# Attention's output rows transposed later and into another bank, the maxima sent from ScalarE, and the variance one tap earlier

## The chip, the cores and the metric

The kernel runs on one core of one Trainium2 chip. The metric is the device time of one execution in microseconds (us), the median over runs. TensorE (PE) multiplies, VectorE (DVE), ScalarE (ACT) and GpSimd (POOL) do elementwise work, SyncE (SP) issues transfers. Each engine runs its own instruction list in order and waits on semaphores for the others.

## What is computed

The input is x, four images of 96 channels and 128 x 128 pixels, float32. Two layers follow each other. Cut to what matters:

```python
# layer 0
xn = layernorm over the 96 channels of each pixel
qk, vs = conv1x1(xn, qk_w), conv1x1(xn, vs_w)            # q, k: 48 channels each, vs: 96
local = depthwise 3x3 conv(vs)
v1, v2 = vs[:, :48], vs[:, 48:]
q, k, v1 = rolled by (-4, -4), cut into 8 x 8 windows, 4 heads of 12 channels
y = softmax(q k^T / sqrt(12)) v1                          # 64 x 64 per window and head
y = concat([windows put back and rolled back, v2])
ca = sigmoid(fu2(leaky_relu(fu1(mean over the image of (y + local)))))
z = conv1x1(y * ca + local * (1 - ca), proj_w) + x
# layer 1: depthwise conv with 4 taps, whose weights come from the image mean of z
out = conv of z with w(relu(batchnorm(w1 @ mean(z)))) + bias
```

Both layers need a mean over a whole image (for `ca` and for layer 1's weights) before the first row of that image's output can be finished.

## The kernel before

The 128 rows of an image are cut into 16 strips of 8 rows (`NS`), 64 strips in all. A strip goes through two parts.

*Attention* of strip t: x is loaded, transposed (`x_transposed`, L471, in two halves) and its statistics taken (`statistics` L980, `variance` L986 to L994); `rsqrt` (L758, L762) and `rstd_rows` (L483) give the factors by which `normalise` (L1001) makes `xn`. From `xn` come values (`vs_of` L496, copied out by `vs_out` L780) and keys and queries (`keys_queries` L504, copied out by L767 or L1210 and by L773). `scores` (L521) makes q k^T of half of the windows in `banks_s`; `maxima` (L1009) takes row maxima, a reduction for each of the two banks; `max_transposed` (L535) turns them, `maxima_out` (L806 on ScalarE, L1017 on VectorE in the first 16 strips) negates them into `nmx`, and SyncE's `move_max` (L281) sends them into rows 62 to 65 of `qd`, where they serve as extra rows of the next product. `scores_transposed` (L529) makes k q^T minus the maxima in both banks of `banks_t`, `exps` (L811) exponentiates from there into `pt`, `values` on TensorE (L558) multiplies by `vd` into `ps_o` (first half) or bank 0 of `banks_t` (second half), `divide` (L1024, L1026) normalises into `yq`. `y_transposed` (L541) transposes `yq` into `ps_o`, ScalarE's `y_out` (L799, four copies, and L801) copies it into `ybuf`, SyncE's `store_y` (L296) writes it to DRAM as `y_img`. The values go to DRAM as `v_img` through GpSimd (L434).

*Mixing* of strip u = t - 17 (`LAG`), one image behind: SyncE's `load_strip` loads `vin`, `ycat`, rows of `mixed` and x0, seven transfers; ScalarE's `first` (L837) and six taps on VectorE (`mix`, L1181) make the local convolution, `project` and `project_mixed` (L612, L614, L619) multiply into `banks_g`, `finish` (L1204) adds x0 and writes `zs`, ScalarE's `tap0` (L847) and three taps on VectorE (`l1`, L1192) make layer 1, and `store_out` writes the result.

The order of instructions on each engine is written out by hand: `alone` for the first 16 strips (attention alone), `strip` for the 48 in which both parts overlap and for the 16 of mixing alone that follow (the last of these on VectorE by `last`). `gate` marks the strip after an image's last, in which the sums over the image are taken (`image_sums` on ScalarE, L882 and L883, `local_mean` and `squeeze_in` on VectorE, from L1108), `gated` the strip after it, in which the image's weights are made.

What orders the work around the change, within one overlapped strip:

- TensorE: x transposes first half, transposed scores first half (waits for `mx_moved`), values' projection (waits for `zs_done`), `y_transposed(t - 1)`, transposed scores second half (waits for the first exponentials), x transposes second half, keys and queries, weighted sums first half, `rstd_rows`, scores first half, project first half, scores second half (waits for the first maxima), weighted sums second half, `max_transposed`, project second half, values transposed, `project_mixed`.
- ScalarE: exponentials first half, `vs_out`, `y_out(t - 1)`, exponentials second half, keys, `rsqrt`, queries, `tap0`, sums of x, `maxima_out`, `first`, values.
- VectorE: `finish`, statistics first half, three taps, statistics second half, variance, two taps, divide, normalise, maxima first half, one layer 1 tap, maxima second half, last tap, divide, two layer 1 taps.
- SyncE: store of the output, `store_y(t - 1)`, two loads of x, two stores of values, `load_strip`, `move_max`.

## Time and profile before

| | |
|---|---|
| runs, median | 1499.13 us (1495.72 to 1505.75, 3 runs) |
| the profiled execution's own time | 1503.79 us, its span 1502.2 us |
| mean granted TensorE clock | 0.984 |
| strips of attention alone | the first 16, to about 300 us |
| strips with both parts | 48, to about 1307 us |
| strips of mixing alone | the last 16 |

The profile is one execution. A line of the timeline gives the start and the duration of an instruction or a run of equal ones, the engine, the line of the kernel, and in brackets how long the engine idled before it and which instruction released it. PEld is TensorE's loading of weights, which overlaps its multiplying. The granted clock is a share of 2.4 GHz.

### The profile page before, as it was taken

The page shows a single profiled execution, that of the slowest core. Times are in us where ns is not written, and L with a number is a line of the kernel's source. Part 1 is how long each engine was busy: PE and PEld are TensorE (multiplying, and loading weights), DVE is VectorE, ACT ScalarE, POOL GpSimd, SP SyncE. Part 2 cuts the span into 40 slices and gives each one's busy share as a digit, 9 for nine tenths or more (in the row PEclk, how much of TensorE's full clock was granted, in tenths as well). Part 3 has the DMA queues.
Part 4 walks back from the last instruction along what each step waited for, and adds up shares of the span by engine and source line. Part 5 has one row for each costly group of instructions (what it writes and reads, how often), then busy time and mean ns, then how long its engine had stood idle before and what let it go on. Part 6 is the DMA issues. An engine that isn't in the chain of part 4 may idle for free.

```text
span 1502.2 us, 38208 instructions
## 1 busy us (share of the span) xinstructions
PE 1323.6 (88%) x12403; PEld 782.0 (52%) x12403; DVE 1263.8 (84%) x2222; ACT 875.8 (58%) x2279; POOL 230.8 (15%) x741
## 2 busy tenths in 40 slices
PE   5989898889899999989899999988989998888986
PEld 3666666555555555555555555555555555433332
DVE  3565656479999999999999999999989998999998
ACT  2566666666666666776566666765666666622221
POOL 2111111111122211221111211220112011000000
PEclk9999999999999999999999999999999999999999
DMA  2121212345665566645655566646655664678884
GB/s 62 51 82 55 81 55 81 99 98 148 167 148 144 138 152 165 156 114 154 166 147 139 138 159 156 156 114 159 155 125 141 161 155 112 164 181 195 211 199 126
DMA packets 81357, 203.07 MB, mean 135 GB/s; under 512 B 15248, under 2 KB 19112, under 8 KB 81320
## 3 DMA queue, kind: packets, MB, share of 16 engines
q1 hardware_dynamic: 81320, 202.60, 53.9%
q8 instruction: 20, 0.33, 0.1%
q14 instruction: 17, 0.14, 0.0%
HBM read 136.57 MB, written 64.91 MB: 134 GB/s over the span
## 4 chain that ended last, share of the span: by engine, by line
PE 36%; ACT 20%; DVE 16%; issue 13%; DMA 13%; ACTq 1%; DVEq 0%; SPq 0%; POOL 0%; POOLq 0%
DMA qd<-nmx 12%; PE banks_s L521 9%; ACT pt L811 5%; PE banks_t L529 5%; PE banks_t L483 5%; ACT km L767 4%; DVE mx L1009 4%; ACT ybuf L799 4%; PE banks_g L612 4%; PE banks_g L496 4%; DVE mixed L1181 3%; PE banks_g L614 3%; DVE oo L1192 3%; ACT vw L780 2%; DVE zs L1204 2%
## 5 line engine op out<-in xcount | busy, mean ns | idle before, releaser
L1181 DVE SCALAR_TENSOR_TENSOR mixed<-vin,c_pack,mixed 96x1024 f32<-96x1024 f32 x352 | 450.0, 1278 | 6.6
L1192 DVE SCALAR_TENSOR_TENSOR oo<-zs,l_w,oo 96x1024 f32<-96x1024 f32 x192 | 245.1, 1276 | 8.3 <-ACT oo L847 4.1
L811 ACT ACTIVATE pt<-banks_t 128x512 f32<-128x512 f32 x256 | 138.6, 593 | 129.0 <-PE banks_t L529 127.5
L1009 DVE TENSOR_REDUCE mx<-banks_s 128x8 f32<-128x512 f32 x260 | 167.6, 687 | 48.1 <-PE banks_s L521 47.3
L529 PE MATMUL banks_t<-qd,km 64*128 64x128 f32 x2048 | 152.8, 290 | 30.1 <-DMA qd<-nmx 30.0
L521 PE MATMUL banks_s<-km,qd 64*128 64x128 f32 x2080 | 152.9, 286 | 18.9 <-issue 15.2
L980 DVE BATCH_NORM_STATS2 bn<-banks_a 128x6 f32<-128x96 f32 x528 | 99.0, 249 | 80.5 <-PE banks_a L471 80.1
L521 PEld LDWEIGHTS banks_s<-km,qd 64*128 64x128 f32 x2080 | 129.7, 189 | 70.7 <-DVE mx L1009 40.4
L612 PE MATMUL banks_g<-vin,proj_t 128*96 128x512 f32 (+1 forms) x288 | 150.2, 622 | 11.4 <-DMA ycat<-y_img 5.7
L529 PEld LDWEIGHTS banks_t<-qd,km 64*128 64x128 f32 x2048 | 127.9, 192 | 49.9 <-issue 26.1
L434 POOL COPY vrow<-vw 96x16 f32<-96x16 f32 (+2 forms) x520 | 153.4, 349 | 0.0
L847 ACT ACTIVATE oo<-zs,c_pack,l_w 96x1024 f32<-96x1024 f32 x64 | 79.0, 1235 | 125.7 <-DVE zs L1204 125.7
L429 POOL TENSOR_TENSOR idle<-idle 96x1 f32<-96x1 f32 x65 | 34.2, 527 | 767.2 <-ACT vw L780 767.2
L789 ACT ACTIVATE vd<-banks_a 64x192 f32<-64x192 f32 x260 | 86.8, 334 | 109.9 <-PE banks_a L510 104.8
L496 PE MATMUL banks_g<-xn,c_pack 96*96 96x512 f32 x260 | 136.6, 650 | 5.7 <-DVE zs L1204 4.4
L504 PE MATMUL banks_g<-xn,w_qk 96*32 96x512 f32 x1040 | 126.8, 605 | 0.0
L483 PE MATMUL banks_t<-ident,rstd 128*96 128x128 f32 x528 | 72.2, 281 | 50.0 <-ACT rstd L762 31.7
L614 PE MATMUL banks_g<-ycat,proj_c 128*96 128x512 f32 x224 | 115.3, 596 | 0.0
L619 PE MATMUL banks_g<-mixed,proj_m 128*96 128x512 f32 x224 | 109.2, 610 | 1.6 <-DVE mixed L1181 1.6
L806 ACT ACTIVATE nmx<-banks_s 32x128 f32<-32x128 f32 x48 | 12.8, 266 | 163.4 <-PE banks_s L535 163.4
L780 ACT ACTIVATE vw<-banks_g,vs_bias 96x512 f32<-96x512 f32 x130 | 88.6, 682 | 27.2 <-PE banks_g L496 22.9
L799 ACT ACTIVATE ybuf<-banks_a 48x256 f32<-48x256 f32 x256 | 93.9, 370 | 4.2 <-PE banks_a L541 2.7
(148 smaller groups left out, 1842.5 us busy)
## 6 DMA issues: line engine op xcount, KB each, us to landing
vin<-v_img SPq DMA_DIRECT2D x64, 495.0 KB, 5.9
v_img<-vrow SPq DMA_DIRECT2D x130, 198.0 KB, 2.8
xc<-in_x SPq DMA_DIRECT2D x134, 192.0 KB, 2.6
x<-in_x SPq DMA_DIRECT2D x64, 384.0 KB, 7.2
out<-oo SPq DMA_DIRECT2D x64, 384.0 KB, 3.0
y_img<-ybuf SPq DMA_DIRECT2D x128, 99.0 KB, 2.0
ycat<-v_img SPq DMA_DIRECT2D x64, 198.0 KB, 4.9
ycat<-y_img SPq DMA_DIRECT2D x64, 198.0 KB, 7.0
```

The lines of the kernel that those rows point to most:

```text
L434: nc.gpsimd.tensor_copy(dst.rearrange("c r (p x) -> c p r x", x=min(WS, src.shape[-1])), src).then_inc(vrow_done, 1)
L483: last = nc.tensor.transpose(bc_bank(c)[:C, j * W:(j + 1) * W], rstd[:, at:at + 1].to_broadcast([128, C]), ident[:])
L496: mm(banks_g[:C, w, :], wvs[:], windows(w), start=True, stop=True).then_inc(vs_done, 1)
L521: last = mm(banks_s[:, t, e * 128:(e + 1) * 128], operand(qd, t, k, p), operand(km, t, k, p), start=True, stop=True, tile_position=(64 * t ...
L529: last = mm(banks_t[:, n, e * 128:(e + 1) * 128], operand(km, n, k, p), operand(qd, n, k, p), start=True, stop=True, tile_position=(64 * n ...
L612: mm(z, proj_t[:rows, n, :], vin[:rows, par, at:at + 4, 1 + dw:1 + dw + W], start=n == 0, stop=False)
L614: mm(z, proj_c[:], ycat[:, par, 4 * c:4 * c + 4, 0:W], start=False, stop=False)
L799: fn(dst, src[:, :, wi, :, :], ACT.Copy, accum_out=ystat[0:A, bass.ds(4 * t + 2 * g + wi, 1)]).then_inc(y1_done, 1)
L811: fn(pt[:, 2 * r + n, :], banks_t[:, n, :], ACT.Exp).then_inc(pt_done, 1)
L1009: v.tensor_reduce(mx[:, n, :, 4 * r:4 * r + 4].rearrange("q h e -> q e h"), banks_s[:, n, :].rearrange("q (e h k) -> q e h k", h=2, k=K), ...
L1181: v.scalar_tensor_tensor(out=mb[:C, par, :, 0:W], in0=vin[:C, par, 1 + dh:1 + dh + WS, 1 + dw:1 + dw + W], scalar=depth_w[:, DVE_TAPS[m]:D ...
L1192: v.scalar_tensor_tensor(out=oo[:, par, :, :], in0=zs[:, at:at + WS, 1 + dw:1 + dw + W], scalar=l1_w[:, n:n + 1], in1=oo[:, par, :, :], op ...
```

## The change

It has six parts.

1. `y_transposed(t - 1)` moves on TensorE from behind the values' projection to behind the second half of the weighted sums, ahead of `max_transposed`, and writes bank 1 of `banks_t` in place of `ps_o`. `yq` gets two buffers. The wait on `y1_done` moves from `values` to ahead of the transposed scores' first half. In overlapped strips the second half of the x transposes takes the free place, ahead of the second half of the transposed scores.
2. `y_out` moves on ScalarE to behind the sums of x (in overlapped strips also behind `maxima_out`), ahead of the values.
3. In overlapped strips ScalarE itself issues the transfer of the maxima behind `maxima_out`, and SyncE no longer does. In the first 16 strips SyncE still issues it. `store_y` becomes the last item of SyncE's strip (in a `gate` strip it stands ahead of the load of `y_img`).
4. `maxima` is one reduction over both banks in place of two, and its semaphore counts 2 a strip in place of 4.
5. On VectorE the second half of the statistics and the variance go ahead of the third tap, on ScalarE `rsqrt` ahead of the keys.
6. In a `gate` strip ScalarE's image sums go behind `maxima_out` and `y_out`, and VectorE's `local_mean` and `squeeze_in` behind the last layer 1 tap.

The core of the diff:

```diff
-        yq = sb("yq", [128, 4, 2, 64])
+        yq = sb("yq", [128, 2, 4, 2, 64])
...
                 if gate is not None:
+                    if rows is not None:
+                        store_y(rows, 1 - rows_par)
                     sp.wait_ge(y_stored[1], FREE + 32 * (NS // 2) * (gate + 1))
...
-                if y:
+                if y and not attend:
                     store_y(t - 1, 1 - k)
...
-                if attend:
+                if attend and alone:
                     move_max(t + 1, 1 - k)
+                if y and attend and gate is None:
+                    store_y(t - 1, 1 - k)
...
-            def y_transposed(t):
-                pe.wait_ge(vd_done, 4 * (t + 2))
+            def y_transposed(t, k):
                 pe.wait_ge(yq_done, FREE + 2 * (t + 1))
                 for e in range(4):
-                    last = nc.tensor.transpose(ps_o[:, e * 128:(e + 1) * 128],
-                                               yq[:, e, :, :].rearrange("q g c -> q (g c)"), ident[:])
+                    last = nc.tensor.transpose(banks_t[:, 1, e * 128:(e + 1) * 128],
+                                               yq[:, k, e, :, :].rearrange("q g c -> q (g c)"), ident[:])
...
                 vs_of(t + 1)
-                if y:
-                    y_transposed(t - 1)
                 x_transposed(t + 2, k, h + 1, 0)
                 pe.wait_ge(mx_moved, 16 * (t + 1))
                 pe.wait_ge(yq_done, FREE + 2 * t)
+                if not (isinstance(t, int) and t < 2):
+                    pe.wait_ge(y1_done, YO * (t - 1))
                 scores_transposed(k, 0)
...
-                values(t, k, 1, not y)
+                values(t, k, 1)
+                if y:
+                    y_transposed(t - 1, 1 - k)
                 pe.wait_ge(yq_done, FREE + 2 * t + 1)
                 max_transposed(t + 1)
...
                     pe.wait_ge(yq_done, FREE + 2 * t)
+                    pe.wait_ge(y1_done, YO * (t - 1))
                     scores_transposed(k, 0)
                     if prev:
                         pe.wait_ge(zs_done, u)
                     vs_of(t + 1)
+                    x_transposed(t + 2, k, h + 1, 1)
...
                 if attend:
-                    x_transposed(t + 2, k, h + 1, 1)
                     keys_queries(t + 1)
...
-                    values(t, k, 1, not y)
+                    values(t, k, 1)
+                    y_transposed(t - 1, 1 - k)
...
-            def maxima_out(s):
+            def maxima_out(s, k):
                 act.wait_ge(mt_done, s + 1)
                 act.wait_ge(mx_moved, 16 * s)
                 fn(nmx[:], ps_mx, ACT.Copy, scale=-1.0).then_inc(nmx_done, 1)
+                act.wait_ge(nmx_done, s + 1)
+                act.dma_start(qd[62:66, k, :, :, :].rearrange("j p w q -> j (p w q)"), nmx[:]).then_inc(mx_moved, 16)
...
+                    rsqrt(t + 2)
                     keys(t + 1, 1 - k)
-                    rsqrt(t + 2)
                     queries(t + 1, 1 - k)
...
                     sum_x(t + 2, k, h + 1, 0)
                     sum_x(t + 2, k, h + 1, 1)
+                if attend:
+                    maxima_out(t + 1, 1 - k)
+                    y_out(t - 1, 1 - k, h - 1 + k)
                 if gate is not None:
                     image_sums(gate)
-                if attend:
-                    maxima_out(t + 1)
...
-                for n in range(2):
-                    v.tensor_reduce(mx[:, n, :, 4 * r:4 * r + 4].rearrange("q h e -> q e h"),
-                                    banks_s[:, n, :].rearrange("q (e h k) -> q e h k", h=2, k=K),
-                                    AX.X, ALU.max).then_inc(mx_done, 1)
+                v.tensor_reduce(mx[:, :, :, 4 * r:4 * r + 4].rearrange("q n h e -> q n e h"),
+                                banks_s[:, :, :].rearrange("q n (e h k) -> q n e h k", h=2, k=K),
+                                AX.X, ALU.max).then_inc(mx_done, 1)
...
                     mix(u, par, 0, tail)
                     mix(u, par, 1, tail)
+                if attend:
+                    statistics(t + 2, 1)
+                    variance(t + 2)
                 if gated is not None and attend:
                     leaky(gated)
                 if cur:
                     mix(u, par, 2, tail)
-                if attend:
-                    statistics(t + 2, 1)
-                    variance(t + 2)
```

## Rows read from the trace of the kernel before

**Rows 1.** The page: the chain that ended last, by line.

```profile
DMA qd<-nmx 12%; PE banks_s L521 9%; ACT pt L811 5%; PE banks_t L529 5%; PE banks_t L483 5%; ACT km L767 4%; DVE mx L1009 4%; ACT ybuf L799 4%; PE banks_g L612 4%; PE banks_g L496 4%; DVE mixed L1181 3%; PE banks_g L614 3%; DVE oo L1192 3%; ACT vw L780 2%; DVE zs L1204 2%
```

**Rows 2.** Busy time, 665 to 959 us: us, each engine's busy us (x instructions), clock.

```profile
665.00:959.00 294.00, 267.22 (x2646) 159.66 (x2644) 273.22 (x449) 190.63 (x483) 54.65 (x154) 1.00 0.59 149
```

**Rows 3.** Windows of L1181 alone (six taps to a strip): stretch, us, busy us (x).

```profile
328.00:620.00 292.00, 107.51 (x84) 1.00 0.60 149
665.00:959.00 294.00, 107.20 (x84) 1.00 0.59 149
1004.00:1286.00 282.00, 99.57 (x78) 0.98 0.58 144
```

**Rows 4.** Waits, 665 to 959 us: who for whom; us in total, times, longest.

```profile
PE banks_t L529 <- DMA qd<-nmx: 7.4, 12, 1.2
DVE mx L1009 <- PE banks_s L521: 7.0, 15, 0.5
DVE zs L1204 <- PE banks_g L619: 6.6, 14, 0.6
...
DVE bn L980 <- PE banks_a L471: 2.3, 6, 0.7
```

**Rows 5.** Timeline, one strip's end: start, us, engine, line, operation, [idle before <-releaser].

```profile
742.08 1.29 DVE L1009 TENSOR_REDUCE mx<-banks_s 128x8 f32<-128x512 f32 x2 [0.51 <-PE banks_s L521]
...
743.43 0.28 PE L535 MATMUL banks_s<-ident,mx 128*32 128x128 f32 x1 [0.34 <-DVE mx L1009]
...
744.12 0.67 SPq L281 DMA_DIRECT2D qd<-nmx  x1
...
748.18 1.28 DVE L1204 SCALAR_TENSOR_TENSOR zs<-banks_g,z_bias,x 96x1024 f32<-96x1024 f32 x1 [0.56 <-PE banks_g L619]
...
749.55 1.16 PE L529 MATMUL banks_t<-qd,km 64*128 64x128 f32 x16 [1.25 <-DMA qd<-nmx]
```

**Rows 6.** Timeline, the strip after it, up to the first maxima.

```profile
752.44 0.60 PE L541 MATMUL banks_a<-ident,yq 128*128 128x128 f32 x4
...
753.41 0.36 ACT L799 ACTIVATE ybuf<-banks_a 48x256 f32<-48x256 f32 x1
...
755.19 1.08 ACT L811 ACTIVATE pt<-banks_t 128x512 f32<-128x512 f32 x2
...
759.59 1.16 PE L521 MATMUL banks_s<-km,qd 64*128 64x128 f32 x16 [0.33 <-issue]
...
760.78 1.29 DVE L1009 TENSOR_REDUCE mx<-banks_s 128x8 f32<-128x512 f32 x2 [0.25 <-PE banks_s L521]
```

**Rows 7.** Timeline: the maxima's transfer issued, and the product that waits for it.

```profile
279.18 0.68 SPq L281 DMA_DIRECT2D qd<-nmx  x1
...
281.22 2.08 PE L529 MATMUL banks_t<-qd,km 64*128 64x128 f32 x16 [1.36 <-DMA qd<-nmx]
```

**Rows 8.** A window of low clock: us, then busy us by engine, clock.

```profile
1263.00:1270.00 7.00, 6.77 (x26) 3.89 (x28) 3.73 (x3) 2.64 (x6) 0.05 (x1) 0.51 0.02 6
```

**Rows 9.** Timeline: the second statistics' wait just after that window.

```profile
1271.54 0.76 DVE L980 BATCH_NORM_STATS2 bn<-banks_a 128x6 f32<-128x96 f32 x4 [4.74 <-PE banks_a L471]
```

**Rows 10.** Timeline: maxima in a strip where VectorE, not TensorE, is late.

```profile
654.68 1.28 DVE L1009 TENSOR_REDUCE mx<-banks_s 128x8 f32<-128x512 f32 x2
...
657.24 1.29 DVE L1009 TENSOR_REDUCE mx<-banks_s 128x8 f32<-128x512 f32 x2
```

**Rows 11.** Timeline, one strip of the first 16, attention alone.

```profile
204.04 0.28 PE L535 MATMUL banks_s<-ident,mx 128*32 128x128 f32 x1 [0.34 <-DVE mx L1009]
...
209.55 1.08 ACT L811 ACTIVATE pt<-banks_t 128x512 f32<-128x512 f32 x2
```

**Rows 12.** Timeline: ScalarE's image sums, first and last, and VectorE's use of them.

```profile
632.49 0.22 ACT L882 ACTIVATE spare<-vstat 96x32 f32 x1
...
634.33 0.20 ACT L883 ACTIVATE edge<-ecol 96x4 f32 x1
...
637.48 0.15 DVE L1108 TENSOR_TENSOR edge<-edge 96x9 f32<-96x9 f32 x1
```

More of the change, by code:

```diff
@@ L344, in _, with strip @@
             move_max(0, 0)
-            def strip(h, k, attend=True, y=True, ahead=False, prev=False, older=False, gate=None):
+            def strip(h, k, attend=True, y=True, ahead=False, prev=False, older=False, gate=None, alone=False):
                 t = 2 * h + k
@@ L591, in _ @@
             scores(0, 0)
-            pe.wait_ge(mx_done, 2)
+            pe.wait_ge(mx_done, 1)
             scores(0, 1)
@@ L661, in strip @@
                     vs_of(t + 1)
+                    x_transposed(t + 2, k, h + 1, 1)
                 elif prev:
                     pe.wait_ge(zs_done, u - 1 if tail and gated is None else u)
-                if y:
-                    y_transposed(t - 1)
+                if y and not attend:
+                    pe.wait_ge(y1_done, YO * (t - 1))
+                    y_transposed(t - 1, 1 - k)
                 if gated is not None:
@@ L674, in strip @@
                 if attend:
-                    x_transposed(t + 2, k, h + 1, 1)
                     keys_queries(t + 1)
-                    values(t, k, 0, not y)
+                    values(t, k, 0)
                     rstd_rows(t + 2, 0)
@@ L684, in strip @@
                     pe.wait_ge(mid_act, gated + 1)
+                    if not attend:
+                        pe.wait_ge(y1_done, YO * B * NS)
                 if attend:
@@ L912, in strip @@
                     vs_out(t + 1, 1)
-                if y:
+                if y and not attend:
                     y_out(t - 1, 1 - k, h - 1 + k)
@@ L1292, in strip @@
                     l1(u - 1, k, 3)
+                if gate is not None and attend:
+                    local_mean(gate)
+                    squeeze_in(gate)
                 if gated is not None:
```

47 lines of the change are left out of this document (21 added, 26 removed).

## Prediction

> **What bounds the kernel now.** I read the page first, then busy time by stage, the waits of the middle stage, the timeline of one of its strips, and the timeline of the first 16 strips. The page says that the largest item of the chain is no engine but the transfer `qd<-nmx` (12%) [rows 1]. Averages hide three stages: 16 strips of attention alone, 48 in which attention of one image overlaps the mixing of the image before, and 16 of mixing alone. The change acts on the first two.
>
> In the middle stage, six taps make a strip: 84 taps are 14 strips, so a strip takes 292/14 = 20.9 us, then 294/14 = 21.0, then 282/13 = 21.7 [rows 3]. VectorE is busy for 273.2/14 = 19.5 us of the 21.0 and TensorE for 267.2/14 = 19.1 [rows 2]. So the most that any reordering could take out is about 1.5 us a strip. Of VectorE's idle 1.48 us, the waits explain 1.14: before the maxima 7.0, before `zs` 6.6, before the second statistics 2.3, together 15.9/14 [rows 4]. The other 0.34 are small gaps.
>
> These waits have one source upstream, a loop through all engines: maxima, transposed (L535), negated, sent by `qd<-nmx`, transposed scores (L529), exponentials, values and output rows copied on ScalarE, the second exponentials, keys, `rstd`, scores, maxima. In the strip shown the transfer is issued at 744.12 and the product that needs it starts at 749.55, after 1.25 us of idle TensorE [rows 5]; it waits in 12 of 14 strips [rows 4]. Then the output copies stand on ScalarE between the first and the second exponentials from 753.41 to 755.19, 1.78 us [rows 6]. Scores come at 759.59, VectorE waits 0.25 for them [rows 6].
>
> **The transfer.** SyncE issues it behind seven loads of the next strip. The one issued at 279.18, with nothing large ahead of it, let its product start at 281.22, 2.04 us later [rows 7]; the one at 744.12 took 5.43 [rows 5]. The change issues it from ScalarE in the middle stage (SyncE keeps it in the first). I take 2.0 to 4 us, since it no longer stands in SyncE's order; the bound from above is 5.4. TensorE is free for the product about 0.1 us after `zs` starts (749.55 less 1.25), which is 4.2 us after the issue, so anything under 4.2 is hidden. The issue itself costs ScalarE something that before does not show: SyncE's took 0.67 and 0.68 [rows 5, 7]. I take 0.7. Queued behind it are the output rows, `first` and `vd`, and behind these the next strip's exponentials. From 744.1 + 0.3 the sum is 0.7, 1.78, 1.28 for `first` (1024 columns, as a tap) and at most 1.78 for `vd`'s four copies: 749.9. The exponentials could start at 749.5, when the product is no longer late. They are at most 0.4 late, and TensorE needs the first pair (1.08) only after values' projection and x transposes, at about 752: the issue may cost 1.7 before anything waits.
>
> The Trainium skill speaks against this gain (DMA: Bandwidth & Descriptors, Issuing engines are not separate DMA queues): DMAs from SP and ACT interleave on the same 16 engines, and issuing from several saves only sequencer time. Its section Queues, rings and completion order says that each DMA engine takes turns between rows, packet by packet, which would let a 16 KB transfer past a backlog. The trace has no transfer from ScalarE that could decide; the first reading is rival A.
>
> **Output rows off the loop.** Their transposes (L541, 0.60 us [rows 6]) leave the gap between the value product and the second transposed scores and go behind the weighted sums; the second x transposes take their place, and the copies (1.78 us) move behind the maxima. Second statistics and variance go one tap (107.2/84 = 1.28 us [rows 3]) earlier. The scores were ready 11.4 us after `zs` (759.59 less 748.18); without 1.78 and with the product 1.2 earlier they could be at about 9.7, while VectorE's own work brings it to the first maxima no earlier than about 11.8. VectorE becomes late there, by about 2 us, so the waits before the statistics (2.3/14 = 0.16) and before the first maxima go. The wait before the second maxima shrinks: it was 0.5 because the scores of the first half and the two projections behind them were late. In a strip in which VectorE was the late one, the pair started at 654.68 and 657.24 with no wait noted [rows 10], 2.56 apart, which is the 2.5 of its own work. I keep 0.1.
>
> **What it costs.** The transposes now sit where TensorE idled only 0.34 us, waiting for the maxima (L535) [rows 5]. Of 0.60 us, 0.26 is left over, and every projection up to `zs` comes that much later; the pipelined spacing may be less (bounds 0.1 and 0.6). The wait before `zs` grows from 6.6/14 = 0.47 to 0.7. Two banks of `yq` and bank 1 of `banks_t` add waits on `y1_done` that the copies of the strip before satisfy, over 1 us early.
>
> **Merged maxima.** One reduction over 1024 columns replaces two of 512, twice a strip. A pair takes 1.29 us, and another operation over 1024 columns, `zs`, 1.28 [rows 5]: the saving could be nothing. At most it is a small operation's whole time, 0.15 [rows 12]. I take 0.05, so 0.1 a strip.
>
> **Sum, middle stage.** 19.5 - 0.1 busy, 0.34 small gaps, 0.1 and 0.7 of waits: 20.5 us a strip. Against 20.9, 21.0 and 21.7 that is 0.4 x 14 + 0.5 x 14 + 1.2 x 13 = 28 us. The last term holds a mechanism of its own: after idling for the transfer TensorE ran at half rate (2.08 instead of 1.16 us for the same product [rows 5, 7]); the granted clock from 1263 to 1270 was 0.51, the 1.2 GHz level, after an idle wait for the same transfer [rows 8], and VectorE then stood 4.74 us [rows 9]. I count two such strips in the third stretch, whose clock is 0.98 against 1.00 in the others [rows 3]. With the transfer early, both go.
>
> **Sum, other parts.** First 16 strips: the transposes fill 0.34 us of idle before L535 [rows 11] and leave their old place, and the exponentials at 209.55, which stood behind the output copies, come forward. TensorE's order sets this stage, so I take 0.34 less the unfilled rest, 0.25 (bounds 0.1 and 0.4): 15 x 0.25 = 4 us. The first two overlapped strips both wait for the transfer; the second gets it about 1 us earlier: 2 us. Two strips at an image's end lose: the image sums (632.49 to 634.53, 2 us [rows 12]) now stand behind issue and output copies, VectorE's mean waits for them, and its small steps no longer lie between taps: 0.5 each, -1 us. SyncE there waits for the output rows before it stores them and loads `y`, which is needed 10 us later. The last 16 strips are untouched.
>
> 28 + 4 + 2 - 1 = 33 us off the profiled execution's own 1503.8 gives 1471. The runs' median is 0.3% lower, 1499.1; 33 off that is 1466, but the two half-rate strips (8 us) may belong to the profiled execution alone. I settle at 1469.
>
> **Rivals.** *A, the transfer stays late.* It lands 5.4 us after its issue as now. The product is still about 1.2 us late, but with the copies gone and two us of reserve this reaches VectorE only through the second statistics, which now stand a tap earlier: about 0.3 us over 41 strips, 12 us: 1481. For it: both queues end in the same engines, whose share is 59% [rows 2]. Against: 2.04 us where nothing was ahead. *B, paid back ahead of `zs`.* If the transposes cost their whole 0.60, so that the serial stretch from second maxima to `zs` (6.1 us in rows 5) grows to 6.7, and 0.3 of wait is left before the second maxima, a strip is 20.5 + 0.3 + 0.2 = 21.0. Then -1, 0 and 9 us come from the three stretches and 5 from the other parts, 13 us: 1486, or 1491 if the half-rate strips are the profiled execution's alone; I put 1489. For it: TensorE has 93% of a 20.5 us strip. Against: its idle 0.34 in just that place. *C, slower.* TensorE now runs ahead of VectorE, and its waits could gather in one place ahead of the scores. Half rate followed an idle stretch of 1.36 [rows 7]; one costs about 4.5 us of a strip. It decides from about seven strips more than now (33/4.5); for over 1% slower, eleven: 1515. Against: at 20.5 us all TensorE's idle together is 1.4, in three places of at most 0.7.
>
> **Chances and range.** Forecast 0.66, A 0.12, B 0.16, C 0.06. A 1% difference (15 us) is about what a measurement can tell. Faster by over 1%: forecast, and most of A, 0.78; within 1%: B, 0.16; slower 0.06. The range goes from 1455 (a strip at 20.3, 0.4 gained in the first stage) to 1488, where A and a half of B end; B's rest and C are left out.
>
> **What would show it.** Right: no idle before L529 for the transfer; 20.4 to 20.6 us between `zs`; waits before statistics and first maxima gone, before the second under 0.2, before `zs` 0.6 to 0.8; no clock under 0.9 after 350 us. Wrong: an issue on ScalarE over 1.7 us, exponentials late by it, or waits ahead of `zs` over 1 us.

## The result: slower by 1.1%, and the profile after

| | before | after |
|---|---|---|
| median of 13 runs each | 1500.8 us (1495.72 to 1508.32) | 1518.62 us (1506.93 to 1537.8) |
| ratio | | 1.0112, 95% interval 1.0083 to 1.0140 |
| the profiled execution | 1503.79 us | 1527.75 us |
| its mean granted clock | 0.984 | 0.953 |

The highest run of the kernel after, 1537.8 us, is a slow one and is left out of the ratio. Forecast was 1469 us, in a range from 1455 to 1488. The time is on the other side. The two profiled executions are 24 us apart, the medians 18: the table by stages below shows a larger loss than the usual one.

In the profile after, the chain that ended last gives the transfer less, 8% for 12% [rows 1], and the statistics (L991), which wait for TensorE's transposes, appear in it:

```profile
DVE mixed L1191 12%; DMA qd<-nmx 8%; PE banks_g L500 7%; PE banks_s L525 6%; PE banks_t L559 4%; DVE bn L991 4%; PE banks_g L508 4%; PE banks_t L533 4%; PE banks_g L620 3%; PE banks_g L613 3%; DVE oo L1202 3%; DVE mx L1019 3%; PE banks_g L615 3%; PE banks_t L487 3%; PE banks_t L544 2%
```

The windows of the three overlapped stretches (columns as in [rows 2]) show that they no longer resemble each other. The first keeps full clock; the second and third fall to 0.95 and 0.94, and VectorE's busy time falls from 273.22 [rows 2] to 256.50, since fewer strips fit into the same window:

```profile
328.00:620.00 292.00, 273.48 (x2716) 165.97 (x2720) 275.04 (x436) 198.98 (x500) 63.73 (x157) 1.00 0.61 152
665.00:959.00 294.00, 264.63 (x2493) 158.37 (x2497) 256.50 (x405) 181.17 (x456) 68.76 (x149) 0.95 0.57 140
1004.00:1286.00 282.00, 258.74 (x2436) 155.14 (x2435) 248.48 (x393) 177.09 (x447) 63.27 (x139) 0.94 0.57 140
```

The waits from 665 to 959 us, which answer to [rows 4]. The maxima's wait is gone (7.0 to 1.4), `zs` waits about as before (7.7 for 6.6), but TensorE waits 20.1 us for the transfer instead of 7.4, in 11 strips and for up to 2.7, and the second statistics 23.3 instead of 2.3:

```profile
DVE bn L991 <- PE banks_a L475: 23.3, 8, 3.9
...
PE banks_t L533 <- DMA qd<-nmx: 20.1, 11, 2.7
...
DVE zs L1214 <- PE banks_g L620: 7.7, 13, 0.7
...
DVE mx L1019 <- PE banks_s L525: 1.4, 3, 0.6
```

A strip in which all goes well, in the timeline. The transfer is issued at 748.78 and its product starts 4.12 us later without a wait. `zs` follows again after 20.13 us:

```profile
748.78 0.64 ACTq L816 DMA_DIRECT2D qd<-nmx  x1
...
752.85 1.28 DVE L1214 SCALAR_TENSOR_TENSOR zs<-banks_g,z_bias,x 96x1024 f32<-96x1024 f32 x1 [0.70 <-PE banks_g L620]
752.90 1.16 PE L533 MATMUL banks_t<-qd,km 64*128 64x128 f32 x16
...
757.41 3.02 POOL L438 COPY vrow<-vw 96x256 f32<-96x256 f32 x8
...
758.75 2.79 DVE L1191 SCALAR_TENSOR_TENSOR mixed<-vin,c_pack,mixed 96x1024 f32<-96x1024 f32 x2
```

A strip that takes 23.55 us, and what it hands to the next. Here x0's load is issued 0.11 us ahead of the maxima. The product waits 2.66 us, then runs in 2.00 instead of 1.16 (the granted clock from 707 to 711 us is 0.57), the values' projection in 2.73 instead of 1.93, VectorE stands 3.37 before its second statistics, and GpSimd's eight copies take 5.07 instead of 3.02. SyncE's loads of the next strip stand behind the store of these copies, so that the next x0 load again comes only 0.73 us ahead of the next maxima:

```profile
700.12 0.32 SPq L322 DMA_DIRECT2D x<-in_x  x1
700.23 0.64 ACTq L816 DMA_DIRECT2D qd<-nmx  x1
...
704.27 1.28 DVE L1214 SCALAR_TENSOR_TENSOR zs<-banks_g,z_bias,x 96x1024 f32<-96x1024 f32 x1 [0.67 <-PE banks_g L620]
...
707.05 2.00 PE L533 MATMUL banks_t<-qd,km 64*128 64x128 f32 x16 [2.66 <-DMA qd<-nmx]
708.99 2.73 PE L500 MATMUL banks_g<-xn,c_pack 96*96 96x512 f32 x4
...
712.09 0.76 DVE L991 BATCH_NORM_STATS2 bn<-banks_a 128x6 f32<-128x96 f32 x4 [3.37 <-PE banks_a L475]
712.83 5.07 POOL L438 COPY vrow<-vw 96x256 f32<-96x256 f32 x8
713.75 3.94 DVE L1191 SCALAR_TENSOR_TENSOR mixed<-vin,c_pack,mixed 96x1024 f32<-96x1024 f32 x3
...
719.86 0.34 SPq L311 DMA_DIRECT2D vin<-v_img  x1
...
723.23 0.32 SPq L322 DMA_DIRECT2D x<-in_x  x1
...
723.96 0.64 ACTq L816 DMA_DIRECT2D qd<-nmx  x1
```

Cut by the starts of `zs` in the timelines, the executions divide as follows. The first column ends at the sixteenth issue of the maxima; a stretch is 14 strips; a pair is the `gate` strip (after an image's last) with the `gated` one behind it; the last column takes all that is left of the execution's own time. The rows below "after" belong to the experiments that follow.

| us | alone | first pair | stretch 1 | pair | stretch 2 | pair | stretch 3 | rest |
|---|---|---|---|---|---|---|---|---|
| before | 264.3 | 63.9 | 291.7 | 45.2 | 293.9 | 45.5 | 303.0 | 196.3 |
| after | 262.7 | 69.4 | 282.8 | 48.9 | 309.3 | 52.3 | 306.8 | 195.6 |
| e15, part 5 undone | 262.4 | 69.4 | 283.3 | 51.9 | 284.3 | 50.5 | 284.4 | 199.1 |
| e5, loads first | 262.4 | 66.3 | 282.4 | 52.0 | 282.5 | 48.6 | 282.3 | 195.9 |
| e3, x0 late | 258.4 | 68.6 | 283.2 | 51.7 | 283.3 | 50.4 | 283.0 | 195.9 |
| b1, before with x0 late | 260.7 | 63.4 | 287.5 | 45.2 | 288.0 | 45.2 | 287.5 | 200.1 |
| e9, e3 with the mean moved | 262.5 | 63.4 | 283.2 | 47.8 | 283.3 | 49.4 | 283.1 | 196.1 |
| e14, e9 with leaky earlier | 261.9 | 62.0 | 282.5 | 46.8 | 282.5 | 45.4 | 282.4 | 198.3 |

After against before: -1.6, +5.5, -8.9, +3.7, +15.4, +6.8, +3.8 and -0.7, together +24.0. Thirteen of the 28 strips of stretches 2 and 3 take 22.7 to 25.0 us, the other fifteen 20.0 to 21.2. The first stretch has none of them. Before each of the thirteen x0's load is issued 0.11 to 0.73 us ahead of the maxima and the product waits 1.69 to 2.85 us; of the other fifteen strips one waits 1.94, one 1.46 and the rest under 0.9. The row of e15 is from the slowest of its four runs (1485.3 us, median 1477.13).

### The profile page after: what moved, and what is told of

Same layout as the page of the kernel before. It is cut to its first block, busy times and chain, and to the rows that moved or that the text cites. A ratio compares the mean times of both kernels' runs of the same rounds, so it can differ in the third digit from the quotient of the medians.

```text
span 1525.9 us, 38002 instructions
## 1 busy us (share of the span) xinstructions
PE 1359.1 (89%) x12403; PEld 806.4 (53%) x12403; DVE 1255.1 (82%) x2092; ACT 882.6 (58%) x2279; POOL 281.6 (18%) x741
## 4 chain that ended last, share of the span: by engine, by line
PE 45%; DVE 30%; issue 11%; DMA 8%; ACT 5%; DVEq 1%; ACTq 0%; SPq 0%; POOL 0%; POOLq 0%
DVE mixed L1191 12%; DMA qd<-nmx 8%; PE banks_g L500 7%; PE banks_s L525 6%; PE banks_t L559 4%; DVE bn L991 4%; PE banks_g L508 4%; PE banks_t L533 4%; PE banks_g L620 3%; PE banks_g L613 3%; DVE oo L1202 3%; DVE mx L1019 3%; PE banks_g L615 3%; PE banks_t L487 3%; PE banks_t L544 2%
## 5 line engine op out<-in xcount | busy, mean ns | idle before, releaser
L438 POOL COPY vrow<-vw 96x16 f32<-96x16 f32 (+2 forms) x520 | 210.4, 460 | 0.0
L533 PE MATMUL banks_t<-qd,km 64*128 64x128 f32 x2048 | 163.8, 304 | 43.7 <-DMA qd<-nmx 41.8
L1019 DVE TENSOR_REDUCE mx<-banks_s 128x16 f32<-128x1024 f32 x130 | 158.8, 1222 | 35.7 <-PE banks_s L525 32.8
L991 DVE BATCH_NORM_STATS2 bn<-banks_a 128x6 f32<-128x96 f32 x528 | 99.0, 249 | 103.3 <-PE banks_a L475 103.2
L533 PEld LDWEIGHTS banks_t<-qd,km 64*128 64x128 f32 x2048 | 137.7, 204 | 60.8 <-issue 49.3
L500 PE MATMUL banks_g<-xn,c_pack 96*96 96x512 f32 x260 | 154.2, 723 | 11.4 <-DVE zs L1214 10.1
L433 POOL TENSOR_TENSOR idle<-idle 96x1 f32<-96x1 f32 x65 | 12.5, 192 | 812.4 <-ACT vw L788 812.4
L613 PE MATMUL banks_g<-vin,proj_t 128*96 128x512 f32 (+1 forms) x288 | 149.9, 621 | 10.5 <-DMA ycat<-y_img 6.7
L807 ACT ACTIVATE ybuf<-banks_t 48x256 f32<-48x256 f32 x256 | 95.1, 374 | 104.2 <-PE banks_t L544 59.3
L508 PE MATMUL banks_g<-xn,w_qk 96*32 96x512 f32 x1040 | 131.8, 626 | 3.1 <-ACT vw L788 3.0
L475 PEld LDWEIGHTS banks_a<-ident,xc 96*128 96x128 f32 x528 | 62.0, 151 | 90.2 <-issue 84.8
L781 ACT ACTIVATE qd<-banks_g,q_bias,q_scale 128x512 f32<-128x512 f32 x130 | 93.9, 776 | 8.6 <-PE banks_g L508 8.6
```

The lines of the kernel that those rows point to most:

```text
L438: nc.gpsimd.tensor_copy(dst.rearrange("c r (p x) -> c p r x", x=min(WS, src.shape[-1])), src).then_inc(vrow_done, 1)
L500: mm(banks_g[:C, w, :], wvs[:], windows(w), start=True, stop=True).then_inc(vs_done, 1)
L508: last = mm(banks_g[q0:q0 + 32, at, :], w_qk[:, kind, t, :], windows(w), start=True, stop=True, tile_position=(0, q0))
L533: last = mm(banks_t[:, n, e * 128:(e + 1) * 128], operand(km, n, k, p), operand(qd, n, k, p), start=True, stop=True, tile_position=(64 * n ...
L613: mm(z, proj_t[:rows, n, :], vin[:rows, par, at:at + 4, 1 + dw:1 + dw + W], start=n == 0, stop=False)
L991: last = v.bn_stats(bn6[:, c, j, :], ps_ln[:, j * C:(j + 1) * C])
```

## The experiments

The theory to test (called L in what is quoted) had two halves. The transfer of the maxima, from whichever queue, lands with x0's load of 384 KB that was issued before it. And the load is late because SyncE stood behind the store of GpSimd's copies, which a late product delays and three taps in a row stretch. The rivals: ScalarE's queue itself is slow (Q), or the loss lies elsewhere. A side question is whether half rate is most of what a bad strip loses (H).

**e1: VectorE's half of part 5 undone.**

```diff
                     mix(u, par, 1, tail)
-                if attend:
-                    statistics(t + 2, 1)
-                    variance(t + 2)
...
                     mix(u, par, 2, tail)
+                if attend:
+                    statistics(t + 2, 1)
+                    variance(t + 2)
```

> The changed kernel with one part undone: on VectorE the second statistics and the variance stand behind the third tap again. Theory L (late loads): in the changed kernel three taps in a row follow the variance, GpSimd's eight copies of the values fall beside them and take 5.06 us instead of 2.0 to 3.0, the store of the values and the loads of the next strip behind it on SyncE are late, and the maxima's transfer is issued 0.7 us after the load of x instead of 2.3 or more; it lands with that load, TensorE idles over 2 us and runs at half rate. Then here the copies take 2 to 3 us, the load of x is issued over 2.3 us ahead of the transfer, at most five strips are over 22 us, and the time is 1470 to 1490. Theory Q (ScalarE's queue itself is served late): nothing changes, 1510 to 1525.

Measured: 1544.6 us, ratio 1.0275 (1.0230 to 1.0320). The half that was wanted came: the copies took 3.0 to 3.1 us in nearly every strip, the load was issued over 3 us ahead of the maxima in nearly all and the product started 4.1 us after the issue. The time didn't follow, for another reason. I had left ScalarE's order as it was, with `rsqrt` ahead of the keys, and it now waits for the variance. Keys, queries and scores are late, TensorE idles 1.64 us and runs the scores in 2.08, and VectorE waits for them. Strips take 21.1 or 22.7 us, against an expectation of at most five over 22:

```profile
419.49 0.30 ACT L766 ACTIVATE lnv<-var,eps 128x8 f32<-128x8 f32 x1 [1.61 <-DVE var L1005]
...
422.88 2.08 PE L525 MATMUL banks_s<-km,qd 64*128 64x128 f32 x16 [1.64 <-issue]
...
424.99 1.23 DVE L1019 TENSOR_REDUCE mx<-banks_s 128x16 f32<-128x1024 f32 x1 [1.28 <-PE banks_s L525]
```

So this run decides nothing on part 5. It shows that its two edits must go together. The experiment is made rightly in e15.

**e2: SyncE issues the transfer in every strip.**

```diff
-                act.dma_start(qd[62:66, k, :, :, :].rearrange("j p w q -> j (p w q)"), nmx[:]).then_inc(mx_moved, 16)
...
-                if attend and alone:
+                if attend:
                     move_max(t + 1, 1 - k)
```

> The changed kernel with one part undone: SyncE issues the maxima's transfer in all strips, behind the loads of the next strip. Theory L: which engine issues it makes no difference to when it lands, 6.5 to 7.7 us after the issue of the load of x ahead of it, so the same strips go wrong: 1510 to 1530. Theory Q: the waits for the transfer go, 1470 to 1485.

Measured: 1532.23 us, ratio 1.0206 (1.0161 to 1.0252). The same pattern, with the load issued 0.83 us ahead and the product 6.40 after the issue:

```profile
794.27 0.32 SPq L322 DMA_DIRECT2D x<-in_x  x1
795.10 0.68 SPq L281 DMA_DIRECT2D qd<-nmx  x1
...
801.50 1.16 PE L533 MATMUL banks_t<-qd,km 64*128 64x128 f32 x16 [2.23 <-DMA qd<-nmx]
802.59 3.63 PE L500 MATMUL banks_g<-xn,c_pack 96*96 96x512 f32 x4
```

For when the transfer lands the queue makes no difference, and Q falls. The time is 0.9% above the kernel after's, outside both intervals. The profiled executions are only 4 us apart and show 5 of it in the pairs, where SyncE sends the maxima behind the load of `y_img`; the rest wasn't traced.

**e3: x0's load held until the maxima have landed.** In overlapped strips `load_strip` leaves out x0, and SyncE ends the strip with it:

```diff
+                if ahead and attend:
+                    sp.wait_ge(mx_moved, 16 * (t + 2))
+                    load_x0(t - LAG + 1, k, prev)
```

> The changed kernel, with the load of x for the mixing part (384 KB) held back on SyncE until the maxima's transfer has landed. Theory L: the transfer lands less than 4.1 us after its issue in every strip, no wait of TensorE for it over 0.3 us outside the first two overlapped strips, no half rate but around the strips at an image's end, 20.2 us a strip: 1470 to 1482. Theory Q: the transfer is as late as in the changed kernel, 1505 to 1525.

Measured: 1473.76 us, ratio 0.980 (0.976 to 0.984). All ordinary strips take 20.13 to 20.40 us, and TensorE doesn't wait for the transfer in any. SyncE could issue the load at 762.26, so the transfer of 759.17 had landed within 3.09 us, with the other six loads still ahead of it:

```profile
759.17 0.64 ACTq L824 DMA_DIRECT2D qd<-nmx  x1
...
762.26 0.32 SPq L327 DMA_DIRECT2D x<-in_x  x1
...
763.27 1.16 PE L541 MATMUL banks_t<-qd,km 64*128 64x128 f32 x16
```

With this load out of the way the transfer is on time. It isn't the load alone that it stands behind, but the burst of seven (1671 KB together) that the load ends. The page gives x0's load 6.8 us from issue to landing in the kernel after and 3.5 here. And in a `gate` strip of e2, where five of the other six had been out for 9 us and more, x0's load went out at 639.62, 0.38 us ahead of the maxima, and the product started 4.04 after their issue, not 6 to 7:

```profile
640.00 0.69 SPq L281 DMA_DIRECT2D qd<-nmx  x1
...
644.04 2.08 PE L533 MATMUL banks_t<-qd,km 64*128 64x128 f32 x16 [5.76 <-DMA qd<-nmx]
```

**b1: the same edit in the kernel before.**

> The kernel before, and nothing of the change, with the load of x for the mixing part held back on SyncE until the maxima's transfer has landed. If the transfer's wait is most of what the loop lost (theory L), the waits of TensorE for it go, the two half-rate strips too, a strip takes 20.5 to 20.6 us: 1475 to 1483, and the change's reordering adds 0.3 us a strip to that. If the output copies between the exponentials keep the loop as long as it was (theory O), the strips stay at 20.8 to 21.0: 1490 to 1498.

Measured: 1477.01 us, ratio 0.9828 (0.9785 to 0.9871). Strips fall from 20.8, 21.0 and 21.6 to 20.5 to 20.6. The load's place is worth more than the whole change, in a kernel that still has the output copies between its exponentials. Against b1, e3 gains 4.3 to 4.7 us in each stretch, 2.3 in the first stage and 4.2 in the rest, and loses 5.2, 6.5 and 5.2 in the pairs: the change as such, freed of the load, is worth 3 us, which is within the uncertainty of the two ratios. Without the rest it would lose 1. Of the rest's 4.2 us, 3.6 lie in one strip at the start of the mixing alone (20.06 for 16.47 us), for which I have no cause.

**e10: e3, with SyncE issuing the transfer.**

> The changed kernel with the load of x held back (e3_x0_late) and the maxima's transfer issued by SyncE in all strips. Theory L: with that load behind it the transfer lands in time from either engine, 1471 to 1477. Theory Q or a worth of ScalarE's queue of its own: waits for the transfer come back, 1482 or more.

Measured: 1478.93 us, ratio 0.9844 (0.9797 to 0.9890). Ordinary strips 20.13 to 20.36, as in e3. Part 3, the issue from ScalarE, is worth nothing in an ordinary strip. The 5 us above e3 are within the uncertainty.

**e7: TensorE kept busy.** In the kernel after, the first x transposes are made six times over, so that TensorE isn't idle while it waits for the transfer.

```diff
-                for j in range(4):
+                for j in [0, 1, 2, 3] * reps:
```

> The changed kernel with the first half of the x transposes made six times over in each overlapped strip, ahead of the transposed scores, so that TensorE works for 2.7 us where it would idle for the maxima's transfer. The transposed scores are then late by 2.3 us or more in every strip, but after work. Theory H (the half rate, not the wait, is most of a bad strip's 3.5 us): no stretch of the overlapped strips away from an image's end has a granted clock under 0.9, the wait before the second statistics is 1.2 to 2.0 us in all strips, none over 2.3, strips of 21.5 to 22.2 us. Theory W (the wait is the loss, the rate adds little): strips that were bad stay at 23.5 us and more.

Measured, one run: 1522.18 us, mean clock 0.989. The windows of the three stretches stay at full clock, although in all but the first strip of stretches 2 and 3 the load goes out 0.5 to 0.7 us ahead of the maxima and the product starts 5.7 to 6.9 us after their issue:

```profile
328.00:620.00 292.00, 283.49 (x2900) 180.52 (x2897) 269.53 (x419) 188.66 (x479) 78.23 (x154) 1.00 0.58 145
665.00:959.00 294.00, 281.21 (x2860) 179.35 (x2859) 264.91 (x415) 187.56 (x474) 77.07 (x151) 1.00 0.57 142
1004.00:1286.00 282.00, 267.78 (x2728) 170.68 (x2725) 254.62 (x408) 179.47 (x455) 70.59 (x143) 1.00 0.58 145
```

Strips take 20.5 to 22.4 us. All pay for the added transposes: the stretches are 295.2, 300.5 and 300.6 us, where the kernel after has 282.8, 309.3 and 306.8, so the sum is no better. It shows the size of the clock's part. Against 20.2 us a bad strip of the kernel after loses 2.5 to 4.8, in the mean 3.7. Here, with the transfer as late and the added transposes on top, no strip of stretches 2 and 3 loses over 2.2, and the mean is 1.3. That speaks for H, as far as one run can.

**e5: the loads ahead of the stores of the values.**

```diff
-                    store_v(t + 1, 1 - k)
...
                     load_strip(t - LAG + 1, k, prev, gate, t - 1 if attend else None, k)
+                if attend:
+                    store_v(t + 1, 1 - k)
```

> The kernel after, with one edit: SyncE issues load_strip's seven loads ahead of the stores of the values, which wait for GpSimd's copies. Theory (the maxima's transfer lands with x0's load, and this load is late because SyncE stood behind GpSimd's copies, stretched to 5 us beside three taps in a row): the load is issued 3 us or more ahead of the maxima in all strips, no wait for the transfer over 0.5, ordinary strips 20.1 to 20.4, the time 1474 to 1482. Rival (the queue is deep in any case and the place of the loads in it makes no difference): transfers still 5 to 7 us in half of the strips, 1510 to 1525. A second rival: the values, stored later, reach the mixing late and the wait moves to the values' rows; then waits for v_img's loads appear.

Measured: 1473.08 us, ratio 0.9825 (0.9802 to 0.9849). The load goes out 9.4 us or more ahead of the maxima, and every ordinary strip takes 20.12 to 20.24 us. TensorE waits for no transfer from 665 to 959 us, so the second rival falls too:

```profile
710.20 0.32 SPq L322 DMA_DIRECT2D x<-in_x  x1
...
719.79 0.64 ACTq L817 DMA_DIRECT2D qd<-nmx  x1
...
723.89 1.16 PE L534 MATMUL banks_t<-qd,km 64*128 64x128 f32 x16
```

The number of bytes is the same; only the distance of the loads from the transfer differs. This is the other end of what e3 does. It also cuts one link of the loop, with part 5 in place: the loads no longer stand behind GpSimd's copies, and no strip goes bad.

**e15: part 5 undone on both engines**, the load where the change leaves it. It is e1 and this:

```diff
-                    rsqrt(t + 2)
                     keys(t + 1, 1 - k)
+                    rsqrt(t + 2)
                     queries(t + 1, 1 - k)
```

> The kernel after with part 5 undone on both engines (second statistics and variance behind the third tap on VectorE, rsqrt behind the keys on ScalarE); x0's load stays ahead of the maxima. The first experiment undid it on VectorE alone. Theory (the loop feeds itself through GpSimd's copies, which take 5.06 us only beside the three taps that part 5 puts in a row): the copies take 3.0 to 4.4 us in every strip, the load is issued 2.3 us or more ahead of the maxima, the product waits at most 0.9 us, TensorE does not fall to half rate, ordinary strips 20.2 to 20.6 in all three stretches: 1473 to 1482. Rival (the load late by itself, from the later images' slower issue of seven loads, is enough): half of the strips of stretches two and three stay at 22.7 to 25, 1500 to 1520, and part 5 has no share in the loss.

Measured: 1477.13 us, ratio 0.9834 (0.9805 to 0.9863). One part of six taken back turns 1.1% slower into 1.7% faster. The load is issued 2.2 to 2.3 us ahead of the maxima in most strips, as in the kernel before (2.32 in [rows 5]'s strip), and a late product no longer makes the next one later. The granted clock is 1.00 in windows of all three stretches. In the strip shown the product waits 1.05 (at most 1.17 in any; 0.9 was expected), runs at full rate, and the copies behind it take 3.00:

```profile
721.56 0.32 SPq L322 DMA_DIRECT2D x<-in_x  x1
...
723.84 0.64 ACTq L816 DMA_DIRECT2D qd<-nmx  x1
...
729.04 1.16 PE L533 MATMUL banks_t<-qd,km 64*128 64x128 f32 x16 [1.05 <-DMA qd<-nmx]
...
733.46 3.00 POOL L438 COPY vrow<-vw 96x256 f32<-96x256 f32 x8
```

**e11: part 5 undone in e3**, with e15's two edits.

> The kernel after with x0's load held, and part 5 undone on both engines: second statistics and variance behind the third tap on VectorE, rsqrt behind the keys on ScalarE. It says what part 5 is worth once the transfer is out of the way, and whether the order of ScalarE was what cost in the first experiment. Theory (part 5 matters only through GpSimd's copies, and these no longer hold the load): ordinary strips 20.1 to 20.4 as with part 5, 1472 to 1480. Rival (the early variance carries the gain of the ordinary strips): strips 20.6 to 20.9, rsqrt late, 1490 to 1500. Copies of GpSimd should take 3.0 us here and 5.1 with part 5.

Measured: 1470.91 us, ratio 0.9806 (0.9770 to 0.9842). Ordinary strips 20.0 to 20.5 against e3's 20.13 to 20.40: with the load out of the way part 5 does neither good nor harm. That copies take 5.1 us with it was wrong: they take 3.0 in e3 too. They meet three taps only when they begin late, so long copies are the loop's second link, not its first.

**e12: e3 with two reductions again.**

```diff
-                v.tensor_reduce(mx[:, :, :, 4 * r:4 * r + 4].rearrange("q n h e -> q n e h"),
...
+                for n in range(2):
+                    last = v.tensor_reduce(mx[:, n, :, 4 * r:4 * r + 4].rearrange("q h e -> q e h"),
...
+                last.then_inc(mx_done, 1)
```

> The kernel after with x0's load held, and part 4 undone: maxima as two reductions over 512 columns, signalled behind the second. It measures the merged reduction alone: 1.22 us against a pair's 1.29. Expected 0.06 to 0.08 us more for each of two pairs a strip where VectorE sets the end: 0.14 a strip, 42 to 63 strips, so 1478 to 1483. Rival (hidden behind TensorE): no difference, 1473 to 1475.

Measured: 1475.6 us, ratio 0.9846 (0.9811 to 0.9881), within the uncertainty of e3. The stretches are 1.1 to 1.7 us longer, 0.1 a strip. The group of the page, in e12 and then in the kernel after: a pair takes 1.27 to 1.29 us end to end (684 ns is the mean of one, with overlap), the merged one 1.222. The expected 1478 to 1483 us didn't come:

```profile
L1028 DVE TENSOR_REDUCE mx<-banks_s 128x8 f32<-128x512 f32 x260 | 167.1, 684 | 30.9 <-PE banks_s L533 27.6
```

```profile
L1019 DVE TENSOR_REDUCE mx<-banks_s 128x16 f32<-128x1024 f32 x130 | 158.8, 1222 | 35.7 <-PE banks_s L525 32.8
```

**e9: the image's mean later.** e3, with `local_mean` and `squeeze_in` moved from the end of the `gate` strip to behind the first statistics of the `gated` one. The reason stands in the timeline of the kernel after. The mean waits 1.61 us for ScalarE's sums, `zs` queues behind it, TensorE idles 3.20 before the values' projection and then makes it at half rate (3.73 for its four products):

```profile
636.09 0.16 DVE L1118 TENSOR_TENSOR edge<-edge 96x9 f32<-96x9 f32 x1 [1.61 <-ACT edge L893]
...
638.24 1.28 DVE L1214 SCALAR_TENSOR_TENSOR zs<-banks_g,z_bias,x 96x1024 f32<-96x1024 f32 x1 [0.15 <-DVE st L1135]
...
639.58 1.17 PE L500 MATMUL banks_g<-xn,c_pack 96*96 96x512 f32 x1 [3.20 <-DVE zs L1214]
```

```diff
                 if attend:
                     statistics(t + 2, 0)
+                if gated is not None and attend:
+                    local_mean(gated)
+                    squeeze_in(gated)
```

> The changed kernel with the load of x held back as in the run before (e3_x0_late), and VectorE's small steps for the image mean taken out of the end of the strip after an image's last and put behind the first statistics of the strip after that. The two strips at an image's end take 23.4 and 28.4 us there, 21.8 and 23.5 in the kernel before. If VectorE's wait for the sums and the steps behind it, in which TensorE has nothing to do, bring on the half rate, the pair goes from 51 to about 45 us, and the time from 1474 to 1460 to 1466. If the late exponentials behind ScalarE's sums are the cause, it stays within 4 us of 1474.

Measured: 1467.71 us, ratio 0.9773 (0.9725 to 0.9821). The `gate` strip is an ordinary one, 20.14 us; the pair is 47.8 and 49.4 for e3's 51.7 and 50.4, short of the 45 that was expected. What is left sits in the `gated` strip: the second small product waits 2.42 us for `leaky`, behind the variance, and keys and queries run at half rate.

```profile
637.58 0.32 PE L608 MATMUL banks_s<-tr,r_pack 24*96 24x1 f32 x2 [2.42 <-DVE tr L1149]
637.84 3.03 PE L516 MATMUL banks_g<-xn,w_qk 96*32 96x512 f32 x16
```

**e14: e9, and `leaky` one tap earlier.**

```diff
                     mix(u, par, 0, tail)
+                if gated is not None and attend:
+                    leaky(gated)
+                if cur:
                     mix(u, par, 1, tail)
```

> The kernel after, with x0's load held until the maxima have landed, the image's mean taken behind the first statistics of the strip after the gate, and leaky one tap earlier, ahead of the second tap and the second statistics. Theory (the pairs at an image's end are lost by single small waits that let TensorE idle over 1.3 us, after which it runs at half rate): fu2's one_column no longer waits 2.42 us; keys and queries then run at about 1.5 instead of 3.03 us; the three pairs shrink from 47.8 and 49.4 us to 45 to 46, and the time from 1467.7 to about 1460. Rival (the pairs are bound by VectorE's small operations themselves, some 20 of 0.15 to 0.23 us): the pairs stay at 47 to 49, 1466 to 1468.

Measured: 1463.02 us, ratio 0.9767 (0.9737 to 0.9797), the fastest of all here. The pairs are 46.8 and 45.4, where the kernel before has 45.2 and 45.5. The product no longer waits, and keys and queries run at full rate. In the first of these two pairs the next wait came up, 1.65 before the scores and 1.10 before the first projection, which then takes 1.76 us (the granted clock from 640.5 to 642.5 us is 0.58):

```profile
632.35 0.32 PE L608 MATMUL banks_s<-tr,r_pack 24*96 24x1 f32 x2
632.61 1.92 PE L516 MATMUL banks_g<-xn,w_qk 96*32 96x512 f32 x16
...
638.29 1.16 PE L533 MATMUL banks_s<-km,qd 64*128 64x128 f32 x16 [1.65 <-issue]
640.55 1.76 PE L621 MATMUL banks_g<-vin,proj_t 128*96 128x512 f32 x2 [1.10 <-ACT proj_t L920]
```

## Why the prediction was wrong

**Where the time would be, and what a strip costs: right.** The forecast was 20.5 us for a strip without the waits. The first stretch takes 282.8/14 = 20.2 and the clean strips 20.13 and 20.23. The waits before the maxima went, the one before `zs` became 0.50 and 0.67 (forecast 0.6 to 0.8), and the issue on ScalarE costs 0.64: the output copies behind it wait 0.9, and nothing waits for them in turn. "Anything under 4.2 is hidden" holds too: products that start 4.09 to 4.12 us after the issue have no wait. That e3, at 1474 us, comes near the 1469 of the forecast doesn't bear out the reordering, though: b1 has 1477 with none of the change. Most of the forecast gain hung on the transfer.

**The step that failed: "The transfer. I take 2.0 to 4 us, since it no longer stands in SyncE's order; the bound from above is 5.4."** It took 5.9 to 7.0 in the bad strips. The bound was read from a strip in which x0's load had been issued 2.32 us ahead of the maxima (741.80 and 744.12, the latter in [rows 5]), and I took that distance as fixed. Steadier is another sum. From the load's issue to the product it is 749.55 - 741.80 = 7.75 in that strip, 6.93 in the bad strip of the kernel after, 7.23 in e2's and 7.48 in e15's; in all strips of the kernel after that wait it is 6.4 to 7.7, in the kernel before 5.7 to 8.6. So what the load comes later, TensorE waits longer. The sum isn't exact, since x0's load only ends the burst. In two strips the seven loads went out over 4.26 us (kernel before) and 4.58 (e15), not 3.4, and the product came 5.65 and 5.88 after x0's load. From the first of the seven it is 9.9 and 10.5 there, and 9.7 to 11.1 in the kernel after.

Nor was 5.4 a bound in the kernel before. In its two half-rate strips the load was 2.13 and 2.31 us ahead, and the product came 5.98 and 6.26 after the maxima's issue. The second of them:

```profile
1256.97 0.67 SPq L281 DMA_DIRECT2D qd<-nmx  x1
...
1263.23 2.08 PE L529 MATMUL banks_t<-qd,km 64*128 64x128 f32 x16 [2.07 <-DMA qd<-nmx]
```

Rival A named the mechanism ("both queues end in the same engines") and priced it at 0.3 us a strip, because it too kept the distance.

**The step that was missing: what the move of the statistics does to GpSimd.** I costed part 5 only on VectorE, where it is neutral. No term named GpSimd's eight copies, although SyncE's stores and all seven loads queue behind them. In the kernel before, a product that is late by up to 1.25 us [rows 5] makes the copies begin as the third tap ends, beside statistics and variance, and they take 2.0. In the kernel after, three taps in a row stand where late copies fall: 5.06. That adds 2 us to the loads, the load comes 0.7 instead of 2.3 us ahead, the product is late by 1.7 to 2.9, the next copies too. e15 and e5 show the links by their absence. In e15 everything but part 5 is there, a distance of 2.2 to 2.3 in most strips and waits up to 1.17 included, and no ordinary strip is over 20.8; in e5 part 5 is there and the loads don't stand behind the copies. The prediction weighed the change as a shorter loop and didn't ask what a late turn of it now meets.

**Half rate: the forecast "with the transfer early, both go" and rival C's "three places of at most 0.7" both fell.** C had the end right, with eleven strips more than now as its price for over 1%; thirteen came in stretches 2 and 3. It was given 0.06, since the idle time was reckoned with the transfer on time. It wasn't an independent case but what A turns into when the wait grows: after 1.25 us of idling the product ran in 1.16 [rows 5], after 1.36 in 2.08 [rows 7], and in the kernel after 2.66 of idling brought 2.00, at a granted clock of 0.57, with the lower level of 1.2 GHz in it. The length of the idling alone doesn't decide: in the kernel before the product ran in 1.16 after 1.32 us, and in e2 after 2.23, with the values' projection behind it slow instead. But in stretches 2 and 3 of the kernel after, no strip with a wait up to 1.46 is over 20.8 us, and of 14 with a longer one 13 take 22.7 and more. A and C should have been one rival, with a chance for the step between them.

**The small terms.** First stage: 4 us forecast, 1.6 came, 0.1 a strip. The first two overlapped strips: 2 us gained forecast, 5.5 lost. The two later pairs: 1 us lost forecast, 3.7 and 6.8 lost. The prediction had the waits ("VectorE's mean waits for them") but priced them as 0.5 of VectorE's time and not as 3.2 us of TensorE's idling followed by half rate; e9 and e14 take most of it back. Merged maxima: 0.1 a strip forecast, 0.1 came. One row was misread without harm: the scores were not ready 11.4 us after `zs` but began there (759.59) and took 1.16 more; VectorE is the late one at the first maxima even so.

**What stays open.** Why the first stretch escapes. There SyncE has its seventh load out 3.0 to 3.2 us behind the first in most strips, in the later stretches 3.4, and the load comes 2.8 to 3.0 us ahead instead of 2.3, with the product on time. What makes the issues slower from the second image on wasn't tried. Nor has part 5 alone in the kernel before a time: with VectorE's half of it that kernel comes to a deadlock. By the order of its code, TensorE in a `gated` strip makes the small product that waits for `leaky` ahead of the second x transposes, and `leaky` would stand behind the statistics of these on VectorE. With `leaky` ahead of them it wasn't tried.

## What to carry to other kernels

Price a transfer by all that was issued shortly before it, on any queue, and ask of each edit whether it moves that distance; look for the longest such time in the trace before calling one a bound. When a step is moved on one engine, look at who runs beside the place that it leaves and the one that it takes, GpSimd beside VectorE above all, and what a late turn of the loop would find there. A wait of TensorE may cost not its length but its length and the products at half rate behind it (in stretches 2 and 3 of the kernel after that came with the waits above 1.5 us); ask how long the longest gets before calling the sum of them small, and move what others wait for ahead of what nobody does.

## What the runs showed of the hardware

A transfer of 16 KB (0.79 MB in 48) from ScalarE's queue, issued 0.1 to 0.7 us behind the last of seven loads on SyncE's (1671 KB, the last 384 KB), lets its product start 6.4 to 7.7 us after that load's issue; from SyncE's own queue, 0.4 to 0.8 us behind, it is 7.0 to 7.7 in ordinary strips. With only the six other loads ahead of it, issued 5.7 to 2.9 us before, it landed within 3.09 us. The Trainium skill (DMA: Bandwidth & Descriptors, Queues, rings and completion order) says that an engine takes turns between queues packet by packet; here that doesn't let a small transfer's completion past a burst of large ones. The same section says that the mark of completion is written only after all earlier writes of the same DMA engine, across its queues. The times fit that, though no run tells it from a plain sharing of the engines.

GpSimd's copies are held up by VectorE's taps. Eight copies take 1.98 to 2.0 us beside statistics and variance, 3.0 with a tap or two beside them, 5.06 beside three. A single one of 96x32 takes 0.20 us at the least and 1.50 at the most within one strip (minimum, median, maximum in ns):

```profile
L438 POOL COPY vrow<-vw x8: 196/425/1503, 712.8 to 717.7; 96x16 f32<-96x16 f32 x4, 96x256 f32<-96x256 f32 x2, 96x224 f32<-96x224 f32 x2
```

The tap beside it takes 1.31 (3.94 for three). The Trainium skill (SBUF — State Buffer, SBUF: two separate sides) has the rule: an operation of VectorE with two inputs in SBUF and one of GpSimd that reads SBUF exclude each other for the whole instruction. A tap reads `vin` and `mixed` and is such an operation; `zs` and the statistics read PSUM. The trace agrees.
